# First layer's attention: the values' products of two heads made together, by query tiles, and w_v split earlier

## The chip, the cores and the metric

One Trainium2 chip, one of its cores. The metric is the device time of one execution in microseconds, the median of several runs. The engines are TensorE (PE; its weight loads are shown apart as PEld), VectorE (DVE), ScalarE (ACT), GpSimd (POOL) and SyncE (SP), which here only issues DMAs.

## The reference

Two transformer-like layers on x of 2 batches x 512 tokens x 512 features, float32. The part that the change touches is the first layer's attention, 32 query heads, 8 key/value heads of 128 features, causal:

```
q, k, v = layernorm(x) @ Wq.T, @ Wk.T, @ Wv.T          # q: 32 heads, k and v: 8 heads
q, k = q * cos + rotate_half(q) * sin, k * cos + rotate_half(k) * sin
scores = q k^T / sqrt(128), masked above the diagonal   # each k head serves 4 q heads
out = softmax(scores) v
x = x + layernorm(out @ Wo.T)
```

After it come a linear layer with low-rank additions, a second attention of 32 heads without a mask, and a gated feed-forward layer. They are unchanged.

## The kernel before, in words

Every matrix product is made of three passes (`product`, L81 to L85): each operand is split into a high part, rounded by ACT, and a low part, the rest (`rest`, L90, a subtraction on DVE or POOL). The passes are hi x lo, lo x hi, hi x hi, accumulated in a PSUM bank; L83, L84 and L85 are their lines.

The first layer's attention runs over 8 groups (one k/v head and its 4 q heads each). A group has 8 slots (2 batches x 4 heads) of 4 query tiles of 128 rows: 32 steps, one score tile each. Scores are causal, so tile t has (t + 1) x 128 columns. The groups' passes are software-pipelined: work of a group goes on into the steps of the next one. Step numbers here are taken within a group, modulo 32; "of eight" means modulo 8, since two slots (a pair) repeat every 8 steps.

What is done at which step is written out in plans. `USES0` places the uses of the two general PSUM banks: q of slot s at 4s - 8, its values' product ("pv") at 4s + 21, k of batch b at 16b - 14 (so at steps 18 and 2), v at 16b + 10, v's transposes at 16b + 14. `OUTS0` places the output projection, 4s + t + 26, `LOADS0` the splitting of weights, `FETCH0` their DMAs, 8 steps ahead. Each engine walks through the steps and does, in a fixed order within a step, what the plans give it; engines wait for each other by semaphores.

One slot's way: TensorE makes q, ACT copies it and swaps its halves for the rope (L1775, L1781, L1782), DVE multiplies by the cosine (L1896), POOL by the sine and adds (L2023, L2027), ACT rounds (L1787), POOL makes the low half. TensorE makes the score tile; DVE adds the mask and takes the minimum (L1938), ACT the exponential (L1825), DVE transposes it in blocks of 32 x 32 into `blocks` (L1957). When both slots of a pair are there, SP moves `blocks` to `moved` by 16 DMAs (L1609), which completes the transposition. Both heads of a pair share one buffer of 4 x 5 blocks: the even slot lies above the diagonal, the odd one below. The landed probabilities are rounded by ACT (`landed_hi`, L1832) and their rest made by DVE (even pieces) and POOL (odd pieces), in eight pieces per pair, of 512, 384, 256 and 128 columns for each slot:

```
for lag, pieces in ((LAND0_AT, (0, 1)), (LAND0_AT + 1, (2, 3))):
    slot = m.slot_at(n, lag)
```

so ACT lands at steps 0, 1, 4 and 5 of eight, and DVE and POOL one step later each. POOL's order within a step is: low half of q or k, landed piece, weight's low half, rope. The values' product of one slot has 4 key chunks k; chunk k serves query tiles k to 3, so its three passes have 512, 384, 256 and 128 columns. DVE scales the bank by the inverse sums (L1886), ACT and DVE split it (L1841, L90), and TensorE projects it by w_out into four output banks, one per query tile, which collect 4 heads and are then added to `acc` by DVE (L1973).

Of the kernel before, what the change touches and what calls it, by code (L numbers as in the profile page):

```python
# [23 lines left out]
P = 128  # L24
# [1130 lines left out]
MOVE0_AT, LAND0_AT, PV0_AT, OUT0_AT = 8, 16, 21, 26  # L1155
# [14 lines left out]
class Linear:  # L1170
# [12 lines left out]
    def __init__(self, p, ctx, ctx0, home, banks, xT, acc, ident, half, x_rows, kept):  # L1183
# [7 lines left out]
        self.x_second = self.blocks[:, 0].rearrange("p g c e i -> p (g c e i)")[:, 0:TB * D]            .rearrange("p (t d) -> p t d", t=TB)  # L1191
# [248 lines left out]
def grouped_attention(p, ctx0, xT, acc, ident, half, x_rows, kept, inv_rows, ahead):  # L1440
# [4 lines left out]
    with ExitStack() as ctx:  # L1445
# [8 lines left out]
        NPR, NRAW, TRIANGLES = 2, 5, [P, 2, TB, TB, TB + 1, 32]  # L1454
# [48 lines left out]
        def by_block(rows):  # L1503
            return rows.rearrange("p (g x) -> p g x", g=TB)

# [6 lines left out]
        def chunk_row(rows, slot, e):  # L1512


            return rows[:, :, e, e + 1:TB + 1] if slot % 2 == 0 else rows[:, :, TB - 1 - e, 0:TB - e]

        def chunk_columns(rows, slot, k):

            if slot % 2 == 0:
                return rows[:, :, k, k + 1:TB + 1]  # L1520
            return rows[:, :, k:TB, k]
# [20 lines left out]
        def landing(m, n):  # L1542

            for lag, pieces in ((LAND0_AT, (0, 1)), (LAND0_AT + 1, (2, 3))):
                slot = m.slot_at(n, lag)
                if slot is not None:
                    for e in pieces:
                        yield slot, e
# [16 lines left out]
        def _(sp):  # L1565
            def fetch(m, x, d):
                kind, h = x
                if m is not start:
                    sp.wait_ge(s_w_hi, m.done(FETCH0, x, d) - NRAW)
                    sp.nop(nofuse=True)  # L1570
                    if not (m.first and d == 0):
                        if kind == "wo":
                            sp.wait_ge(s_out, TT + m.done(OUTS0, (GH + h, TB - 1), d - 1))
# [20 lines left out]
            def move(m, pair):  # L1594
# [16 lines left out]
                wait_past(sp, s_inv_dma, m, 32 * (SLOTS // 2), 32 * pair + 16)  # L1611
                sp.dma_start(inv_all[:, k], inv_rows[k].rearrange("p t -> (p t)").unsqueeze(0).to_broadcast([P, P * PAIR]))\
# [37 lines left out]
        def _(pe):  # L1650
            def bank_use(x, m, d, part=range(C)):
# [10 lines left out]
                if kind == "pv":  # L1662
# [5 lines left out]
                    wait_past(pe, s_lo_even, m, 2 * SLOTS, 2 * slot + 2)  # L1668
                    wait_past(pe, s_lo_odd, m, 2 * SLOTS, 2 * slot + 2)
                    for k in range(TB):  # L1670
                        right = Split(chunk_columns(probsT_hi, slot, k),
                                      chunk_columns(probsT_lo[:, slot // 2 % 2], slot, k))
                        last = product(nc, by_block(bank[:])[:, :, k * 32:P].rearrange("p g (t i) -> p g t i", i=32),
                                       v[:, j // GH, k * HD:(k + 1) * HD], right, k == 0, k == TB - 1)
# [31 lines left out]
            def project(m, x, d):  # L1706

                slot, t = x
                h = slot % GH
                if t == 0:  # L1710
                    wait_past(pe, s_o_lo, m, SLOTS, slot + d * SLOTS + 1)
                    if slot < GH:
                        pe.wait_ge(s_w, m.done(LOADS0, ("wo", h), d))
                if h == 0:
                    wait_past(pe, s_added, m, B * TB, TB * (slot // GH + d * B - 1) + t + 1)
                product(nc, out_bank[t][:], oT[:, slot % 2, t * P:(t + 1) * P], w_out[:, h], h == 0, h == GH - 1)\
# [43 lines left out]
        def _(act):  # L1760
# [60 lines left out]
            def exponentials(m, n):  # L1821
# [4 lines left out]
                               bias=negtop[:, n:n + 1], scale=-1.0, accum_out=total[:, n:n + 1]).then_inc(s_exp, 1)  # L1826

            def landed_hi(m, slot, e):
                pair = slot // 2
                if slot % 2 == 0 and e == 0:  # L1830
                    wait_past(act, s_move[pair % 2], m, SLOTS // 4 * MOVES, (pair // 2 + 1) * MOVES)
                act.activation(chunk_row(probsT_hi, slot, e), chunk_row(moved[:, pair % 2], slot, e), ACT.Copy)\  # L1832
                    .then_inc(s_land_hi, 1)
# [9 lines left out]
            def body(m):  # L1843
                for n in m.steps():
# [16 lines left out]
                    for slot, e in landing(m, n):  # L1861
                        landed_hi(m, slot, e)
# [13 lines left out]
        def _(dve):  # L1876
# [71 lines left out]
            def turn_blocks(m, n):  # L1948
# [7 lines left out]
                to = rows[:, :, 0:t + 1, t + 1] if slot % 2 == 0 else rows[:, :, t, 0:t + 1]  # L1956
                dve.transpose(to.rearrange("p c k i -> p k c i"), probs[:, n % NPR, 0:width[t]]).then_inc(s_block, 1)  # L1957

            def landed_lo(m, slot, e):
                wait_past(dve, s_land_hi, m, TILES, TB * slot + e + 1)  # L1960
                k = slot // 2 % 2
                rest(dve, chunk_row(probsT_lo[:, k], slot, e), chunk_row(moved[:, k], slot, e),
                     chunk_row(probsT_hi, slot, e)).then_inc(s_lo_even, 1)
# [5 lines left out]
            def add_rows(m, x, d):  # L1969
                slot, t = x  # L1970
                dve.wait_ge(s_out, TT + m.done(OUTS0, x, d))
                row = slot // GH * TB + t
                dve.tensor_tensor(acc[:, row], out_bank[t][:], acc[:, row], ALU.add).then_inc(s_added, 1)  # L1973
# [4 lines left out]
            def body(m):  # L1978
                for n in m.steps():
# [22 lines left out]
                    for slot, e in landing(m, n - 1):  # L2002
                        if e % 2 == 0:
# [350 lines left out]
```

## Time and profile before

| | |
|---|---|
| time, median of 3 runs (lowest to highest) | 2220.83 us (2217.11 to 2226.0) |
| the profiled execution | 2219.26 us |
| its span | 2217.4 us |
| granted TensorE clock, mean over the span | 0.979 of full |
| TensorE busy | 2095.7 us, 95% |
| DVE, ACT, POOL busy | 76%, 61%, 55% |

The span is that of the instructions in the profile; the execution's time has a little around it. "Busy" of TensorE comes from modelled ends of pipelined matmuls, so the distance from one start to the next tells more than the length. In a timeline each row has the start (us from the span's start), the length, engine and line, operation, output<-inputs, partitions x elements, and in brackets the idle time before it and the instruction that ended it.

### The profile page before, as it was taken

Reading aid. Unit: us, or ns where it says so; the run is one execution under the profiler, and the core shown is the slowest. Engines: PE = TensorE matmul, PEld = TensorE weight load, DVE = VectorE, ACT = ScalarE, POOL = GpSimd, SP = SyncE. Lnnn points to the kernel's source line nnn. Section 1 sums busy time; section 2 is a strip of 40 time slices with the busy share of each in tenths; the row PEclk is TensorE's granted clock in tenths of the full one; section 3 lists DMA queues with packets and bytes.
Section 4 is the critical chain, followed back from the end, with each engine's and each line's share of the span. In section 5 each row is a group of like instructions: output and inputs, shape, how many; then the busy total and the mean of one; then the engine's idle time right before and its main releaser. Section 6 shows DMA issues by size and latency. Waiting matters only on the chain. (4 is left out here: it accounts for less than half of the span.)

```text
span 2217.4 us, 38457 instructions
## 1 busy us (share of the span) xinstructions
PE 2095.7 (95%) x10535; PEld 1765.5 (80%) x10535; DVE 1674.3 (76%) x2972; ACT 1349.9 (61%) x3637; POOL 1223.1 (55%) x985
## 2 busy tenths in 40 slices
PE   6999999999999778999999999999999999968998
PEld 5788888888887657888888888888888888756787
DVE  5778888788788876888878788787877788885322
ACT  5777777777776456666656565665656565554321
POOL 3878787787786555545444554545454553454300
PEclk9999999999999989999999999999999999988999
DMA  2434344434344422444444444444443443433210
GB/s 82 125 105 125 108 104 119 109 109 122 105 118 125 126 69 75 124 99 117 112 105 102 115 106 118 102 100 111 114 106 95 120 108 93 127 113 100 91 53 25
DMA packets 165904, 231.96 MB, mean 105 GB/s; under 512 B 47281, under 2 KB 77137, under 8 KB 165745
## 3 DMA queue, kind: packets, MB, share of 16 engines
q1 hardware_dynamic: 165744, 229.97, 39.5%
q8 instruction: 83, 1.36, 0.3%
q14 instruction: 77, 0.62, 0.1%
HBM read 114.23 MB, written 6.55 MB: 54 GB/s over the span
## 5 line engine op out<-in xcount | busy, mean ns | idle before, releaser
L90 POOL TENSOR_TENSOR l_probsT_lo<-l_moved,l_probsT_hi 128x512 fp32r<-128x512 f32 (+2 forms) x256 | 282.6, 1108 | 307.7 <-ACT l_probsT_hi L940 279.8
L934 ACT ACTIVATE l_probs<-l_score,l_negtop 128x512 f32<-128x512 f32 x256 | 175.8, 687 | 373.8 <-DVE l_negtop L1045 373.0
L90 DVE TENSOR_TENSOR l_probsT_lo<-l_moved,l_probsT_hi 128x512 fp32r<-128x512 f32 (+1 forms) x256 | 288.8, 1128 | 30.9 <-ACT l_probsT_hi L940 30.9
L1045 DVE TENSOR_REDUCE l_negtop<-l_score 128x1 f32<-128x512 f32 x256 | 175.7, 687 | 91.5 <-PE l_score L85 89.2
L1825 ACT ACTIVATE l_probs<-l_score,l_negtop 128x128 f32<-128x128 f32 (+3 forms) x256 | 134.8, 527 | 178.0 <-DVE l_negtop L1938 176.6
L83 PE MATMUL l_score<-l_kT_lo,l_qT_hi 128*128 128x512 f32 (+3 forms) x512 | 191.7, 374 | 42.0 <-POOL l_qT_lo L90 16.8
L83 PE MATMUL l_out<-l_w_out_lo,l_oT_hi 128*128 128x512 f32 x512 | 208.7, 408 | 3.3 <-DVE l_oT_lo L90 2.6
L1938 DVE CUSTOM_DVE_ANT_0 l_score<-l_score,l_mask 128x128 f32<-128x128 f32 (+3 forms) x256 | 126.3, 493 | 107.2 <-PE l_score L85 106.2
L84 PE MATMUL l_out<-l_w_out_hi,l_oT_lo 128*128 128x512 f32 x512 | 201.3, 393 | 0.0
L85 PE MATMUL l_out<-l_w_out_hi,l_oT_hi 128*128 128x512 f32 x512 | 201.1, 393 | 0.0
L83 PE MATMUL l_general<-l_w_qk_lo,xT_hi 128*128 128x512 f32 x504 | 197.4, 392 | 2.5 <-PEq L1445 2.5
L84 PE MATMUL l_general<-l_w_qk_hi,xT_lo 128*128 128x512 f32 x504 | 197.4, 392 | 0.0
L85 PE MATMUL l_general<-l_w_qk_hi,xT_hi 128*128 128x512 f32 x504 | 197.1, 391 | 0.0
L83 PE MATMUL l_general<-l_probsT_lo,l_v_hi 128*128 128x512 f32 (+3 forms) x512 | 182.6, 357 | 13.4 <-POOL l_probsT_lo L90 7.9
L85 PE MATMUL l_general<-l_probsT_hi,l_v_hi 128*128 128x512 f32 (+3 forms) x512 | 185.3, 362 | 0.0
L84 PE MATMUL l_general<-l_probsT_hi,l_v_lo 128*128 128x512 f32 (+3 forms) x512 | 184.9, 361 | 0.0
L85 PE MATMUL l_score<-l_kT_hi,l_qT_hi 128*128 128x512 f32 (+3 forms) x512 | 184.7, 361 | 0.0
L84 PE MATMUL l_score<-l_kT_hi,l_qT_lo 128*128 128x512 f32 (+3 forms) x512 | 184.2, 360 | 0.0
L1060 DVE STREAM_TRANSPOSE l_blocks<-l_probs 128x512 f32<-128x512 f32 x256 | 177.8, 695 | 0.2 <-ACT l_probs L934 0.2
L90 POOL TENSOR_TENSOR l_w_qk_lo<-l_raw_qk,l_w_qk_hi 128x512 fp32r<-128x512 f32 x60 | 77.6, 1294 | 154.6 <-ACT l_w_qk_hi L908 154.6
L640 ACT ACTIVATE l_squares<-l_y 128x128 f32<-128x128 f32 x512 | 151.9, 300 | 10.6 <-DVE l_y L1003 10.6
L83 PEld LDWEIGHTS l_score<-l_kT_lo,l_qT_hi 128*128 128x128 f32 x512 | 96.9, 189 | 69.7 <-ACT l_probs L1825 20.2
(249 smaller groups left out, 6348.6 us busy)
## 6 DMA issues: line engine op xcount, KB each, us to landing
l_moved<-l_blocks SPq DMA_DIRECT2D x1024, 64.0 KB, 2.0
l_moved<-l_blocks SPq DMA_DIRECT2D x512, 80.0 KB, 2.1
l_inv_all<-inv_rows SPq DMA_DIRECT2D x32, 512.0 KB, 4.3
l_raw_out<-l_wo SPq DMA_DIRECT2D x64, 256.0 KB, 4.5
l_inv_all<-inv_rows SPq DMA_DIRECT2D x64, 256.0 KB, 3.7
l_raw_q<-l_wq SPq DMA_DIRECT2D x32, 256.0 KB, 4.3
l_raw_qk<-l_wq SPq DMA_DIRECT2D x64, 128.0 KB, 3.0
l_raw_qk<-l_wk SPq DMA_DIRECT2D x64, 128.0 KB, 3.0
```

The lines of the kernel that those rows point to most:

```text
L83: nc.tensor.matmul(out, left.hi, right.lo, start=first, stop=False, skip_group_check=True)
L84: nc.tensor.matmul(out, left.lo, right.hi, start=False, stop=False, skip_group_check=True)
L85: return nc.tensor.matmul(out, left.hi, right.hi, start=False, stop=last, skip_group_check=True)
L90: return engine.tensor_tensor(out, full, hi.bitcast(F32), ALU.subtract)
L640: last = act.activation(self.squares[:, h], self.y[:, b, t, h * HD:(h + 1) * HD], ACT.Square, accum_out=self.sumsq[:, b, j:j + 1])
L934: act.activation(probs[:, n % NPR], score[n % 2][:], ACT.Exp, bias=negtop[:, n:n + 1], accum_out=total[:, n:n + 1]).then_inc(s_exp, 1)
L1045: dve.tensor_reduce(negtop[:, n:n + 1], score[n % 2][:], AXX, ALU.max, negate=True)\
L1060: dve.transpose(to, probs[:, n % NPR]).then_inc(s_block, 1)
L1825: act.activation(probs[:, n % NPR, 0:width[t]], score[n % 2][:, 0:width[t]], ACT.Exp, bias=negtop[:, n:n + 1], scale=-1.0, accum_out=total ...
L1938: dve.tensor_tensor_reduce(out=score[n % 2][:, 0:w], in0=score[n % 2][:, 0:w], in1=mask[:, S - w:S], scale=-SCALE, scalar=3.0e38, op0=ALU. ...
```

## The change

A pair's two heads are laid out together in 20 blocks (of 32 columns, times 4) instead of two triangles: blocks 0 to 11 hold query tiles 2 and 3 of both heads for key chunks 0 to 2, blocks 12 to 19 the rest. The even slot's bank now takes query tiles 0 and 1 of both heads, the odd slot's bank tiles 2 and 3 of both. The passes of a pair's products are then 512 and 256 columns (even), and 512, 512, 512, 256 (odd): 18 matmuls instead of 24, with the same columns in sum. Landing is done for the pair, in five pieces of 512 columns: ACT at steps 2 (two), 4 (two) and 5 of eight, DVE pieces 1, 2, 4 and POOL pieces 0, 3 one step later. The output projection takes the heads in the new order, so w_out of odd heads is needed 2 steps and split 1 step sooner, and the additions to `acc` fall in other steps. w_v's split moves from step 4 to step 0. Fetches stand 7 steps ahead of the splits instead of 8. SP's moves wait for TensorE's product (`s_bank`) instead of DVE's scaling (`s_free`), which now only the broadcast of the inverse sums waits for; ACT waits for the pair before's odd product ahead of its first piece.

```diff
-MOVE0_AT, LAND0_AT, PV0_AT, OUT0_AT = 8, 16, 21, 26
+MOVE0_AT, PV0_AT, OUT0_AT = 8, 21, 26
+LAND0_AT = {18: (0, 1), 20: (2, 3), 21: (4,)}
+PIECES0, EVEN0, ODD0 = 5, (1, 2, 4), (0, 3)
...
-LOADS0 = {("wq", h): 4 * h - 13 for h in range(GH)} | {("wo", h): 4 * h + 22 for h in range(GH)}
-LOADS0 |= {("wk", 0): -19, ("wv", 0): 4}
-FETCH0 = Plan({x: n - 8 for x, n in LOADS0.items()})
+LOADS0 = {("wq", h): 4 * h - 13 for h in range(GH)} | {("wo", h): 4 * h + 22 - h % 2 for h in range(GH)}
+LOADS0 |= {("wk", 0): -19, ("wv", 0): 0}
+FETCH0 = Plan({x: n - 7 for x, n in LOADS0.items()})
...
-        NPR, NRAW, TRIANGLES = 2, 5, [P, 2, TB, TB, TB + 1, 32]
+        NPR, NRAW, TRIANGLES = 2, 5, [P, 2, TB, TB * (TB + 1), 32]
...
+        def cells(slot, t):
+            h = slot % 2
+            if t >= 2:
+                return slice(2 * h + t - 2, 4 * t + 2 * h + t - 1, 4)
+            at = (12, 16)[t] + 2 * h
+            return slice(at, at + t + 1)
+
+        def piece(rows, e):
+            return rows[:, :, 4 * e - 8:4 * e - 4] if e >= 2 else rows[:, :, 12 + 4 * e:16 + 4 * e]
+
+        def column(n):
+            slot, t = divmod(n, TB)
+            return slot // 2 * PAIR + (2 * t + slot % 2 if t < 2 else TB + 2 * (slot % 2) + t - 2)
+
+        PV = ([(0, slice(12, 19, 2), slice(0, 4)), (1, slice(17, 20, 2), slice(2, 4))],
+              [(k, slice(4 * k, 4 * k + 4), slice(0, 4)) for k in range(TB - 1)] + [(3, slice(13, 16, 2), slice(1, 4, 2))])
+
+        def out_item(slot, n):
+            return (n % 2, n // 2, n % 2 * 2 + n // 2) if slot % 2 == 0 else (2 + n % 2, n // 2, n)
...
-                if not (m.first and pair < 2):
-                    was = 2 * pair - 3
-                    sp.wait_ge(s_free, m.done(USES0, ("pv", was % SLOTS), was // SLOTS, of_dve))
+                    sp.wait_ge(s_bank, m.done(USES0, ("pv", was % SLOTS), was // SLOTS))
...
-                    for k in range(TB):
-                        right = Split(chunk_columns(probsT_hi, slot, k),
-                                      chunk_columns(probsT_lo[:, slot // 2 % 2], slot, k))
+                    for k, at, to in PV[odd]:
+                        right = Split(probsT_hi[:, :, at], probsT_lo[:, pair % 2, :, at])
...
+            def landed_hi(m, pair, e):
+                if e == 0:
+                    if not (m.first and pair == 0):
+                        was = 2 * pair - 1
+                        act.wait_ge(s_bank, m.done(USES0, ("pv", was % SLOTS), was // SLOTS))
+                        act.nop(nofuse=True)
+                    wait_past(act, s_move[pair % 2], m, SLOTS // 4 * MOVES, (pair // 2 + 1) * MOVES)
+                act.activation(piece(probsT_hi, e), piece(moved[:, pair % 2], e), ACT.Copy).then_inc(s_land_hi, 1)
...
             def add_rows(m, x, d):
-                slot, t = x
-                dve.wait_ge(s_out, TT + m.done(OUTS0, x, d))
+                slot, n = x
+                t, of, _ = out_item(slot, n)
+                if slot % GH // 2 * 2 + of == GH - 1:
+                    dve.wait_ge(s_out, TT + m.done(OUTS0, x, d))
```

## Rows read from the trace of the kernel before

**Rows 1.** The page, part 1: busy time of each engine, its share, instructions.
```profile
PE 2095.7 (95%) x10535; PEld 1765.5 (80%) x10535; DVE 1674.3 (76%) x2972; ACT 1349.9 (61%) x3637; POOL 1223.1 (55%) x985
```

**Rows 2.** Timeline of TensorE at steps 8 and 24: start us, length, instruction, [idle before, releaser].
```profile
312.26 0.32 PE L83 MATMUL l_score<-l_kT_lo,l_qT_hi 128*128 128x128 f32 x1 [1.54 <-POOL l_qT_lo L90]
...
355.36 0.39 PE L85 MATMUL l_general<-xT_hi,l_w_q_hi 128*128 128x512 f32 x1
356.21 0.32 PE L83 MATMUL l_score<-l_kT_lo,l_qT_hi 128*128 128x128 f32 x1 [0.46 <-POOL l_qT_lo L90]
...
399.35 0.39 PE L85 MATMUL l_general<-xT_hi,l_w_q_hi 128*128 128x512 f32 x1
401.27 0.32 PE L83 MATMUL l_score<-l_kT_lo,l_qT_hi 128*128 128x128 f32 x1 [1.54 <-POOL l_qT_lo L90]
```

**Rows 3.** Timeline of TensorE through one value product of before and the next matmuls.
```profile
404.11 0.40 PE L83 MATMUL l_general<-l_probsT_lo,l_v_hi 128*128 128x512 f32 x1
...
404.81 0.34 PE L83 MATMUL l_general<-l_probsT_lo,l_v_hi 128*128 128x384 f32 x1
...
405.34 0.28 PE L83 MATMUL l_general<-l_probsT_lo,l_v_hi 128*128 128x256 f32 x1
...
405.69 0.22 PE L83 MATMUL l_general<-l_probsT_lo,l_v_hi 128*128 128x128 f32 x1
...
405.97 0.45 PE L83 MATMUL l_out<-l_w_out_lo,l_oT_hi 128*128 128x512 f32 x1
406.26 0.40 PE L84 MATMUL l_out<-l_w_out_hi,l_oT_lo 128*128 128x512 f32 x1
```

**Rows 4.** Timeline of ACT from step 18 to step 20.
```profile
342.42 0.58 ACT L1825 ACTIVATE l_probs<-l_score,l_negtop 128x384 f32<-128x384 f32 x1 [2.79 <-DVE l_negtop L1938]
...
344.41 0.60 ACT L1775 ACTIVATE l_rope<-l_general 128x512 f32<-128x512 f32 x1
345.31 0.69 ACT L1825 ACTIVATE l_probs<-l_score,l_negtop 128x512 f32<-128x512 f32 x1 [0.30 <-DVE l_negtop L1938]
...
347.23 0.37 ACT L1825 ACTIVATE l_probs<-l_score,l_negtop 128x128 f32<-128x128 f32 x1
...
349.01 1.05 ACT L1832 ACTIVATE l_probsT_hi<-l_moved 128x512 fp32r<-128x512 f32 x2
```

**Rows 5.** Timeline of POOL from step 21 to the q of step 24.
```profile
350.13 1.37 POOL L90 TENSOR_TENSOR l_probsT_lo<-l_moved,l_probsT_hi 128x384 fp32r<-128x384 f32 x1 [1.20 <-ACT l_probsT_hi L1832]
351.46 1.74 POOL L2023 TENSOR_TENSOR l_rope<-l_rope,l_trig 128x512 f32<-128x512 f32 x1
...
354.61 1.47 POOL L90 TENSOR_TENSOR l_qT_lo<-l_rope,l_qT_hi 128x512 fp32r<-128x512 f32 x1
```

**Rows 6.** Timelines of POOL (first row) and DVE around step 20.
```profile
347.64 1.30 POOL L90 TENSOR_TENSOR l_w_q_lo<-l_raw_q,l_w_q_hi 128x512 fp32r<-128x512 f32 x1
...
345.63 0.68 DVE L1896 TENSOR_TENSOR l_rope<-l_rope,l_trig 128x512 f32<-128x512 f32 x1
...
347.69 1.80 DVE L90 TENSOR_TENSOR l_oT_lo<-l_scaled,l_oT_hi 128x512 fp32r<-128x512 f32 x1
```

**Rows 7.** Groups by form, 150 to 750 us: count, busy us, mean ns, idle before.
```profile
L90 POOL TENSOR_TENSOR l_probsT_lo<-l_moved,l_probsT_hi 128x384 fp32r<-128x384 f32 x55 | 68.9, 1252 | 26.0 <-ACT l_probsT_hi L1832 26.0
...
L1832 ACT ACTIVATE l_probsT_hi<-l_moved 128x512 fp32r<-128x512 f32 x55 | 34.3, 624 | 5.3 <-DMA l_moved<-l_blocks 5.0
```

**Rows 8.** Timeline of POOL from step 5 to the q of step 8.
```profile
394.15 1.24 POOL L90 TENSOR_TENSOR l_probsT_lo<-l_moved,l_probsT_hi 128x384 fp32r<-128x384 f32 x1 [0.35 <-ACT l_probsT_hi L1832]
395.35 1.75 POOL L90 TENSOR_TENSOR l_w_v_lo<-l_raw_v,l_w_v_hi 128x512 fp32r<-128x512 f32 x1
...
399.88 1.26 POOL L90 TENSOR_TENSOR l_qT_lo<-l_rope,l_qT_hi 128x512 fp32r<-128x512 f32 x1
```

**Rows 9.** Timeline of SP's queue, last group's last pair.
```profile
732.52 0.33 SPq L1600 DMA_DIRECT2D inv_rows<-l_inv  x1
734.59 10.88 SPq L1609 DMA_DIRECT2D l_moved<-l_blocks  x16
```

More of the change, by code:

```diff
@@ L1542, in landing @@
         def landing(m, n):
-            for lag, pieces in ((LAND0_AT, (0, 1)), (LAND0_AT + 1, (2, 3))):
+            for lag, pieces in LAND0_AT.items():
                 slot = m.slot_at(n, lag)
-                if slot is not None:
+                if slot is not None and slot % 2 == 0:
                     for e in pieces:
-                        yield slot, e
+                        yield slot // 2, e
         def pair_at(m, n):
@@ L1611, in move @@
                 wait_past(sp, s_inv_dma, m, 32 * (SLOTS // 2), 32 * pair + 16)
+                if not (m.first and pair < 2):
+                    sp.nop(nofuse=True)
+                    sp.wait_ge(s_free, m.done(USES0, ("pv", was % SLOTS), was // SLOTS, of_dve))
                 sp.dma_start(inv_all[:, k], inv_rows[k].rearrange("p t -> (p t)").unsqueeze(0).to_broadcast([P, P * PAIR]))\
@@ L1860, in body @@
                             output_hi(m, x, d)
-                    for slot, e in landing(m, n):
-                        landed_hi(m, slot, e)
+                    for pair, e in landing(m, n):
+                        landed_hi(m, pair, e)
                     for x, d in m.turns(USES0, n, 5):
@@ L1955, in turn_blocks, with landed_lo @@
                 rows = blocks[:, pair % 2]
[L1956 to L1963, printed above, removed]
+                dve.transpose(rows[:, :, cells(slot, t)].rearrange("p c k i -> p k c i"), probs[:, n % NPR, 0:width[t]]).then_inc(s_block, 1)
+            def landed_lo(m, pair, e):
+                wait_past(dve, s_land_hi, m, PIECES0 * SLOTS // 2, PIECES0 * pair + e + 1)
+                k = pair % 2
+                rest(dve, piece(probsT_lo[:, k], e), piece(moved[:, k], e), piece(probsT_hi, e)).then_inc(s_lo_even, 1)
             def output_lo(m, slot):
@@ L2001, in body @@
                             rope_cos(x, m, d)
-                    for slot, e in landing(m, n - 1):
-                        if e % 2 == 0:
-                            landed_lo(m, slot, e)
+                    for pair, e in landing(m, n - 1):
+                        if e in EVEN0:
+                            landed_lo(m, pair, e)
                     for x, d in m.turns(OUTS0, n):
-                        if x[0] % GH == GH - 1:
-                            add_rows(m, x, d)
+                        add_rows(m, x, d)
                     if m.last:
@@ L2032, in rope_lo, with landed_lo @@
                 rest(pool, to.lo, rope[:, rope_at(m, x, d)[0], 0], to.hi).then_inc(s_rope_lo, 1)
-            def landed_lo(m, slot, e):
-                wait_past(pool, s_land_hi, m, TILES, TB * slot + e + 1)
-                k = slot // 2 % 2
-                rest(pool, chunk_row(probsT_lo[:, k], slot, e), chunk_row(moved[:, k], slot, e),
-                     chunk_row(probsT_hi, slot, e)).then_inc(s_lo_odd, 1)
+            def landed_lo(m, pair, e):
+                wait_past(pool, s_land_hi, m, PIECES0 * SLOTS // 2, PIECES0 * pair + e + 1)
+                k = pair % 2
+                rest(pool, piece(probsT_lo[:, k], e), piece(moved[:, k], e), piece(probsT_hi, e)).then_inc(s_lo_odd, 1)
             for t in range(TT):
@@ L2053, in body @@
                             rope_lo(x, m, d)
-                    for slot, e in landing(m, n - 1):
-                        if e % 2:
-                            landed_lo(m, slot, e)
+                    for pair, e in landing(m, n - 1):
+                        if e in ODD0:
+                            landed_lo(m, pair, e)
                     for x, d in m.turns(LOADS0, n, 1):
```

45 lines of the change are left out of this document (17 added, 28 removed).

## The prediction

> **What bounds the kernel now.** I read the page's busy table first: TensorE (PE) is busy for 95% of the span, VectorE (DVE) 76%, ScalarE (ACT) 61%, GpSimd (POOL) 55% [rows 1]. The edit touches only the first layer's attention. Its rhythm can be read from TensorE's timeline: step 8 of two neighbouring groups begins at 312.26 and 401.27, so a group of 32 steps takes 89.0 us, and eight groups take some 712 of the 2217 us [rows 2]. Inside a group matmuls follow each other without a hole except in two places. At step 8 TensorE's last matmul before the score starts at 399.35; one such matmul takes about 0.23, so the score could start at 399.58 and starts at 401.27: 1.69 us lost. At step 24 it is 355.36 + 0.23 = 355.59 against 356.21: 0.62 lost [rows 2]. Both rows name the same releaser, the low half of q, made on POOL. So the layer is bound by TensorE's instruction stream plus two waits on POOL, 2.3 us in every 89. These are the two steps for which k's rope is made as well (k at steps 18 and 2, its rope on POOL at 21 and 5), in front of that q.
>
> **The products.** I take the cadence, start to start, not the modelled durations. In a value product of before, three matmuls of 512 columns take 404.81 - 404.11 = 0.70, three of 384 take 0.53, three of 256 take 0.35, three of 128 take 0.28, and the next one, of 512, is held for 0.29 instead of 0.23, which I charge to the 128s: 0.34. That is 1.92 per head, 3.84 per pair [rows 3]. Three narrow ones thus cost what three of 256 do. The change keeps the columns and regroups them: the even slot's bank takes 3 of 512 and 3 of 256 (0.70 + 0.35 = 1.05), the odd slot's 9 of 512 and 3 of 256 (2.45), together 3.50. TensorE saves 0.34 per pair, 32 pairs, 10.9 us. But the saving is uneven: the even slot's product (steps 5, 13, 21, 29) shrinks by 0.87, the odd one's (1, 9, 17, 25) grows by 0.53. The two losing steps, 8 and 24, lie behind an even product. Whatever POOL does at 5 to 7, TensorE now asks for the q 0.87 sooner, and if POOL is not quicker, that much turns into waiting. The new order reads blocks of 32 columns that lie apart; the old order read such blocks for its odd heads too, so I charge nothing.
>
> **The landing, ACT.** Before, a pair's probabilities were rounded in eight pieces (512, 384, 256, 128 columns for each head) at steps 0, 1, 4, 5 of eight; now in five of 512 at steps 2, 2, 4, 4, 5. Columns are equal and three instructions fall away, but step 2 gains two pieces that it did not have. At step 18 ACT has no room for them: it waits until 342.42 for the score's top, and then runs without a hole: exponential, swap of q, copy of k at 344.41, exponential 19 at 345.31 (after 0.30 of waiting), exponential 20 at 347.23, swap of k, two pieces from 349.01 to 350.06 [rows 4]. Two pieces of 0.62 (the mean of a landing piece of 512, [rows 7]), overlapping by a tenth, make 1.15. Put in ahead of the copy they move it to 345.56 and exponential 19 to 346.1: the 0.30 is used up and 0.8 stays. The next two pieces (512 and 512 for 512 and 384) end 0.1 later still. Here lies the price of the later landing: POOL's piece of step 21 waits for the second of them.
>
> **The landing, POOL and DVE.** At step 21 POOL starts its piece at 350.13, after 1.20 of idle time until ACT delivered, and then has k's two rope instructions and q's low half, which ends at 354.61 + 1.47 = 356.08; 0.13 later the score starts [rows 5]. All of it is in one queue, 5.95 us long. A piece of 512 in place of 384 adds 0.3 (a split of 512 alone takes 1.30, row 347.64 in [rows 6]; the 384s took 1.25 on average, collisions included, in [rows 7], and 1.0 is 1.30 by columns and a fixed part). So with ACT's delay alone q's half comes 0.8 + 0.1 + 0.3 = 1.2 us later. That is the lower bound for this chain. The upper one comes from DVE's new piece at step 3 of eight, which stands ahead of the mask and minimum of the next score. POOL now works on its own new piece at that time (345.05 to 346.35) and then on q's rope. DVE and POOL hold each other up: DVE's oT low half took 1.80 us from 347.69, beginning just after POOL's weight split at 347.64 (1.30 long), against 0.68 for the uncontended cosine of 345.63, and ended 0.55 after POOL did [rows 6]. Taking the same for the new order, DVE's cosine waits to 346.9, POOL's rope runs to 348.2, DVE's piece ends 348.8, the score's minimum 349.2, and exponential 20 starts at 349.3 instead of 347.23. POOL's piece then starts 2.1 later than before; plus 0.3 for its width, less 0.5 for a collision that its rope had (1.74 at 351.46, 1.30 alone) and need not have again: 1.9 [rows 5]. The trace has no row for that order, so both ends are kept: +1.2 to +1.9 at step 24. I take 1.55, between the ends, since the waits are shown but their order in the new kernel is not. The Trainium skill says of this pair (SBUF — State Buffer, "Who interferes with whom") that a VectorE instruction with two inputs in SBUF and a GpSimd instruction that reads SBUF exclude each other for the whole instruction; by that rule the upper end holds, and the trace agrees in the 1.80 us row.
>
> **The sum for the half group with step 24.** TensorE's stretch from score 18 to score 24 grows by 1.2 to 1.9 (its own 0.87 is lost in the longer wait). Steps 17 and 25 add 0.53 each, step 29 saves 0.87. Together +1.4 to +2.1.
>
> **The v weight.** POOL's split of w_v takes 1.75 us at 395.35 and stands between the piece at 394.15 and k's rope, ahead of the q that step 8 waits for, which ends at 399.88 + 1.26 = 401.14 [rows 8]. It goes to step 1, where POOL has no landing any more. So step 8's chain loses 1.75. It gains ACT's and DVE's delay as at step 24 (between 1.0 and 2.1, since POOL waited only 0.35 there), and 0.3 for the wider piece: -0.4 to +0.6. The half group: that, plus 0.53 twice, less 0.87: -0.2 to +0.8. A group thus grows by 1.2 to 2.9, I take 2.0. Seven groups have each chain: +14 us (+8.5 to +20). The first group has no landing at step 8 and so gets the w_v gain alone, and the last has no k rope at 24: together -1 us.
>
> **Costed at nothing.** The moves from blocks to moved are as many and as long (16 issues, 10 to 11 us on SP). They now wait for the product instead of its scaling. In the last group that frees SP at about 732.9 (inv_rows is issued at 732.52) instead of 734.59 [rows 9]: up to -1.7 there, but landing's first pieces come two steps later in a tail of norms on DVE; I set 0, bounds -2 and +2. In the loop their start 4 us sooner covers the weights' fetches, queued behind them on SP: w_v, now needed at step 0 and not 4, is issued after the moves of step 24, and without that head start it would come in the same microseconds as its use. Fetches of wq0 and wo0 wait for output products of the same step, before a move that waits for DVE anyway. ACT's new wait for the odd product stands behind an exponential that needs a later score: covered. The accumulations moved from steps 6 to 9 to 4, 5, 8, 9 add 0.68 before two minimums on DVE; ACT is later still there.
>
> **Result.** The profiled execution took 2219.26 us (span 2217.4 and 1.9 around it); it is 1.6 under the median of 2220.83. 2219.3 + 14 - 1 = 2232; against the median 2234.
>
> **Rivals.** *POOL was the queue, and w_v's removal opens it* (faster). If ACT delivers its pieces of steps 4 and 20 no later than before (POOL waited 0.35 and 1.20 for them), all of w_v's 1.75 is gained (0.53 + 0.53 - 0.87 - 1.75 = -1.56 for that half), and the other half keeps its wait of 0.62 (-0.68): -2.2 per group, 7 groups, -16 us: 2205. For it: the long queue in [rows 8]. Against it: ACT's only idle time from 342.42 to 350.06 is the 0.30 [rows 4]. It decides where ACT's delay is under 0.35. *A wash:* the q of step 24 comes as before relative to score 18 (+0.19), that of step 8 gains half of w_v's 1.75: -0.5 per group, 2217, down to 2212 if all of it. *The port never collides* and step 8's chain is at its low end: +1.2 per group, 2229. *Both instructions exclude each other at every step*, the rule quoted above taken to its end: +2.9 per group, plus small waits at step 0 where q's slack is under 1 us: 2243 to 2249. *It doesn't do what it says* (narrow products cost nothing now): the cadence of 128s, 0.34 for three, excludes it.
>
> **Chances and range.** Forecast (2232 to 2242) 0.46; port at every step (2242 to 2250) 0.14; collision-free (2223 to 2231) 0.20; wash 0.10; faster 0.10. About half a per cent, 11 us, is what a measurement of this kernel can tell from no change. Slower by more: 0.60, within: 0.30, faster: 0.10. The range 2217 to 2249 leaves out the faster rival and half of the wash; the forecast's own is 2232 to 2242.
>
> **What would show it.** Group period 90.2 to 91.9 instead of 89.0; 18 matmuls per pair and none of 128 columns among the value products; the wait before score 24 at 2.5 or more, that before score 8 between 1.2 and 2.5; exponential 20 (of 128 columns) 0.8 to 2 us later behind score 18; DVE's piece at step 19 over 1.2 us long. I am wrong if the waits at 8 and 24 stay at or under 2.3 in sum.

## The result, and the profile after

The changed kernel takes 2250.49 us (median of 4 runs, 2248.6 to 2253.08) against 2220.76 beside it: 1.0134 of before, 95% interval 1.0116 to 1.0152, 30 us slower. The direction was forecast (+14), the size was not: 2234 stood against 2250.5, and the range ended at 2249. The profiled execution took 2250.93 us, its span is 2249.1 ([rows 1] is the same line of before):

```profile
PE 2103.7 (94%) x10343; PEld 1751.7 (78%) x10343; DVE 1689.1 (75%) x2940; ACT 1339.6 (60%) x3541; POOL 1218.1 (54%) x921
```

The 192 matmuls fewer are there. TensorE is busy 8 us longer all the same, which already says that some of its matmuls took longer.

**Where the time went.** The starts of the first layer's 256 score tiles are all in both traces, so each step has an interval, from the start of its score to the start of the next. Means over groups 2 to 6, in us (their sum, "group", is called the period below); steps that are not listed differ by 0.02 at most:

| interval from step | 0 | 1, 17 | 5, 13, 21, 29 | 6, 22 | 7 | 8 | 9 | 15 | 23 | 24 | 25 | 31 | group |
|---|---|---|---|---|---|---|---|---|---|---|---|---|---|
| before | 3.75 | 4.35 | 2.99 | 1.22 | 4.44 | 2.50 | 4.33 | 2.74 | 3.37 | 2.52 | 4.33 | 1.38 | 88.97 |
| after | 3.87 | 4.83 | 2.11 | 2.15 | 5.29 | 3.40 | 4.86 | 3.11 | 5.30 | 4.14 | 5.05 | 2.19 | 96.13 |

A group grew by 7.2 us where 2.0 was forecast. The layer's last score starts at 771.38 instead of 724.83, 46.6 us later. Of this the total shows 30: the second attention layer, which no line of the change touches, became faster. From its first to its last score minimum it takes 1083.2 us instead of 1100.4 (139.3 us in each full group against 141.0 to 143.2). So two effects of opposite sign have to be explained.

**The waits.** TensorE's timeline of after, around step 24 (first five rows) and step 8 of the next group, which answer to [rows 2]:

```profile
368.91 0.50 PE L83 MATMUL l_score<-l_kT_lo,l_qT_hi 128*128 128x512 f32 x1 [0.77 <-ACT l_probs L1842]
...
374.21 0.47 PE L83 MATMUL l_score<-l_kT_lo,l_qT_hi 128*128 128x128 f32 x1 [2.28 <-POOL l_qT_lo L90]
...
375.43 0.63 PE L84 MATMUL l_general<-xT_hi,l_w_q_lo 128*128 128x512 f32 x1
375.86 0.63 PE L85 MATMUL l_general<-xT_hi,l_w_q_hi 128*128 128x512 f32 x1
376.29 0.63 PE L83 MATMUL l_general<-xT_lo,l_w_q_hi 128*128 128x512 f32 x1
...
422.70 0.32 PE L83 MATMUL l_score<-l_kT_lo,l_qT_hi 128*128 128x128 f32 x1 [2.27 <-POOL l_qT_lo L90]
...
423.60 0.40 PE L85 MATMUL l_general<-xT_hi,l_w_q_hi 128*128 128x512 f32 x1
423.83 0.40 PE L83 MATMUL l_general<-xT_lo,l_w_q_hi 128*128 128x512 f32 x1
```

Before both scores TensorE now loses 2.43 us (2.66 from start to start, less 0.23 for a matmul), where before it was 1.69 and 0.62. Such a stretch without a matmul is called a hole below and given from start to start. One step ahead of each TensorE waits for an exponential, which is new. Now read the distance of the matmuls behind the wait: 0.43 us at 375.43, 0.23 at 423.60. After the first of the two equal waits TensorE runs at half its clock for some 3 us, after the second it doesn't. The windows of two neighbouring groups show it as a whole (length, busy times with counts, then the granted clock, the DMA share, GB/s):

```profile
300.30:396.74 96.44, 89.63 (x417) 73.98 (x417) 77.17 (x149) 64.35 (x147) 69.31 (x48) 0.96 0.40 103
396.74:491.68 94.94, 88.14 (x416) 72.65 (x417) 76.52 (x149) 64.23 (x147) 69.30 (x48) 0.98 0.40 105
```

Before, every group from 2 to 6 has granted clock 1.00. In after it falls behind score 24 in all five of them and behind score 8 in three.

**The chain to score 24.** ACT, DVE and POOL of after in the same half group (answering to [rows 4 to 6]):

```profile
358.43 0.58 ACT L1842 ACTIVATE l_probs<-l_score,l_negtop 128x384 f32<-128x384 f32 x1 [2.88 <-DVE l_negtop L1957]
...
360.42 1.15 ACT L1852 ACTIVATE l_probsT_hi<-l_moved 128x512 fp32r<-128x512 f32 x2
361.48 0.58 ACT L1792 ACTIVATE l_rope<-l_general 128x512 f32<-128x512 f32 x1
361.95 0.68 ACT L1842 ACTIVATE l_probs<-l_score,l_negtop 128x512 f32<-128x512 f32 x1
...
364.98 0.37 ACT L1842 ACTIVATE l_probs<-l_score,l_negtop 128x128 f32<-128x128 f32 x1 [1.22 <-DVE l_negtop L1957]
...
366.76 1.16 ACT L1852 ACTIVATE l_probsT_hi<-l_moved 128x512 fp32r<-128x512 f32 x2
...
368.30 0.46 ACT L1842 ACTIVATE l_probs<-l_score,l_negtop 128x256 f32<-128x256 f32 x1
```

```profile
361.64 1.33 DVE L1915 TENSOR_TENSOR l_rope<-l_rope,l_trig 128x512 f32<-128x512 f32 x1
362.90 1.78 DVE L90 TENSOR_TENSOR l_probsT_lo<-l_moved,l_probsT_hi 128x512 fp32r<-128x512 f32 x1
364.60 0.29 DVE L1957 CUSTOM_DVE_ANT_0 l_score<-l_score,l_mask 128x128 f32<-128x128 f32 x1
...
372.22 0.73 DVE L90 TENSOR_TENSOR l_probsT_lo<-l_moved,l_probsT_hi 128x512 fp32r<-128x512 f32 x1
```

```profile
368.00 1.27 POOL L90 TENSOR_TENSOR l_probsT_lo<-l_moved,l_probsT_hi 128x512 fp32r<-128x512 f32 x1 [0.46 <-ACT l_probsT_hi L1852]
369.22 1.75 POOL L2041 TENSOR_TENSOR l_rope<-l_rope,l_trig 128x512 f32<-128x512 f32 x1
371.12 1.28 POOL L2045 TENSOR_TENSOR l_rope<-l_rope 128x512 f32<-128x512 f32 x1
372.37 1.71 POOL L90 TENSOR_TENSOR l_qT_lo<-l_rope,l_qT_hi 128x512 fp32r<-128x512 f32 x1
```

This is the forecast's upper path. Cosine 1.33 and DVE's piece 1.78 us long, where POOL works too (the same piece with 0.73 at 372.22), minimum 20 behind it, exponential 20 1.74 later behind exponential 18 than before (6.55 against 347.23 - 342.42 = 4.81), ACT's pieces at 366.76, POOL's at 368.00, and q's low half ready at 374.08. At 368.30 a price that the forecast left out can be read: exponential 21 stands behind swaps, two pieces and a copy, and score 23 (368.91) needs the bank that it frees.

### The profile page after: what moved, and what is told of

Read it like the earlier page. It is cut to its first block and busy times, and to the rows that moved or that the text cites. A ratio compares the mean times of both kernels' runs of the same rounds, so it can differ in the third digit from the quotient of the medians.

```text
span 2249.1 us, 37941 instructions
## 1 busy us (share of the span) xinstructions
PE 2103.7 (94%) x10343; PEld 1751.7 (78%) x10343; DVE 1689.1 (75%) x2940; ACT 1339.6 (60%) x3541; POOL 1218.1 (54%) x921
## 3 DMA queue, kind: packets, MB, share of 16 engines
HBM read 114.23 MB, written 6.55 MB: 54 GB/s over the span
## 5 line engine op out<-in xcount | busy, mean ns | idle before, releaser
L90 POOL TENSOR_TENSOR l_probsT_lo<-l_moved,l_probsT_hi 128x512 fp32r<-128x512 f32 x192 | 254.9, 1333 | 401.0 <-ACT l_probsT_hi L940 263.8
L90 DVE TENSOR_TENSOR l_probsT_lo<-l_moved,l_probsT_hi 128x512 fp32r<-128x512 f32 x224 | 308.8, 1379 | 32.3 <-ACT l_probsT_hi L940 32.1
L83 PE MATMUL l_general<-l_probsT_lo,l_v_hi 128*128 128x512 f32 x448 | 172.7, 386 | 15.2 <-POOL l_probsT_lo L90 7.9
L84 PE MATMUL l_general<-l_probsT_hi,l_v_lo 128*128 128x512 f32 x448 | 172.0, 384 | 0.0
L85 PE MATMUL l_general<-l_probsT_hi,l_v_hi 128*128 128x512 f32 x448 | 171.5, 383 | 0.0
```

The source lines that it names most:

```text
L83: nc.tensor.matmul(out, left.hi, right.lo, start=first, stop=False, skip_group_check=True)
L84: nc.tensor.matmul(out, left.lo, right.hi, start=False, stop=False, skip_group_check=True)
L85: return nc.tensor.matmul(out, left.hi, right.hi, start=False, stop=last, skip_group_check=True)
L90: return engine.tensor_tensor(out, full, hi.bitcast(F32), ALU.subtract)
```

## Experiments

Layer one's period is the measure below; the total holds the second layer too. Four small edits of a few lines, condensed:

```diff
 # k's rope late (POOL)
-for x, d in m.turns(USES0, n, 3):
-    if x[0] in QK: rope_add(x, m, d)
+for x, d in m.turns(USES0, n, 3):
+    if x[0] == "q": rope_add(x, m, d)
+for x, d in m.turns(USES0, n, 4):
+    if x[0] == "k": rope_add(x, m, d)
 # spread / middle landing
-LAND0_AT = {18: (0, 1), 20: (2, 3), 21: (4,)}
+LAND0_AT = {18: (0, 1), 21: (2,), 22: (3,), 23: (4,)}
+LAND0_AT = {18: (0, 1), 20: (2,), 21: (3,), 22: (4,)}
 # DVE's pieces behind the next minimum
 tops(m, n)
+for pair, e in landing(m, n - 2):
+    if e in EVEN0: landed_lo(m, pair, e)
...
-for pair, e in landing(m, n - 1):
-    if e in EVEN0: landed_lo(m, pair, e)
```

**1. k's rope late, on the kernel after.**

> The kernel after, with POOL making the sine product and the sum of k's rope one step later (steps 22 and 6), so that they stand behind the low half of q that steps 24 and 8 wait for. Theory, the queue on POOL and the clock: in the kernel after TensorE loses 2.43 us before each of these two scores, and in the steps right behind them about 2.7 us per group to a granted clock of 1.2 GHz. Without k's rope (3.0 us) in front, the low half of q is ready about when it is asked for, so both go: group period 96.1 less 4.9 less 2.7 = 88.5 us, and about 2250 - 53 = 2197 in all. Rival one, ACT delivers q's high half too late: the wait stays over 1.5 us and the period over 94. Rival two, the clock falls for the denser stream of 512 columns, waits or not: the waits go, the 2.7 stays, period 91.2, about 2216.

2206.8 us, 0.9944 of before (0.9925 to 0.9963): 44 us less than after. Period 89.7, granted clock 1.00 in the groups. The interval of step 7 falls from 5.29 to 2.85, of 23 from 5.30 to 2.86. So the queue on POOL made the two waits. The 1.2 us over the expected 88.5 is mostly ACT: the waits of 0.93 for its exponential remain, and 0.46 each before scores 9 and 25 appear.

```profile
351.48 1.27 POOL L90 TENSOR_TENSOR l_probsT_lo<-l_moved,l_probsT_hi 128x512 fp32r<-128x512 f32 x1 [0.46 <-ACT l_probsT_hi L1852]
353.46 1.29 POOL L90 TENSOR_TENSOR l_qT_lo<-l_rope,l_qT_hi 128x512 fp32r<-128x512 f32 x1 [0.71 <-ACT l_qT_hi L1804]
```

POOL's timeline there: the low half follows the piece at once, 2.0 us behind it instead of 4.4.

**2. The same on the kernel before.**

> The kernel before, with k's rope one step later on POOL and nothing else. The two waits of before (1.69 and 0.62 us per group) go: period 89.0 less 2.3 = 86.7 us, about 2205 in all. If ACT or DVE set the time of q's low half instead of POOL's queue, the period stays within 0.5 us of 89.

2204.0 us, 0.9921 (0.9904 to 0.9937), period 87.1. As expected, but 0.3 us are lost at each of steps 9 and 25.

**3. The landing spread.**

> The kernel after, with the landing pieces 2, 3 and 4 of a pair at steps 5, 6 and 7 of eight in place of 4, 4 and 5. Theory: ACT's two pieces at step 4 hold back the exponential that frees the bank for the score of step 7 (0.93 us lost there twice per group), and POOL's piece at step 5 stands ahead of q's low half. The first wait goes; TensorE then asks for q 0.93 sooner and POOL has it 1.3 sooner, so that 2.0 of the 2.43 us stay, or about 1.2 if POOL's later instructions also no longer collide. Group period 96.1 less 1.9 less 0.9 to 2.5 = 91.7 to 93.3 with the clock as it is, and 2.7 less of that if a wait of 1.2 no longer lets the clock fall: 89 to 93, 2200 to 2229. Rival, the two pieces are not what the score of step 7 waits for (DVE's minimum is): its wait of 0.93 stays and the period is 94 or more.

A miss: 2335.0 us, 1.0518 (1.05 to 1.0535), period 105.7. The waits of steps 6 and 22 went (1.28), so they hang on ACT's two pieces at step 4 of eight, and those of 8 and 24 shrank; but the odd products' intervals (1, 9, 17, 25) rose from 4.83 to between 8.2 and 10.1, and the granted clock of a group is 0.95. TensorE's timeline:

```profile
405.25 0.32 PE L83 MATMUL l_score<-l_kT_lo,l_qT_hi 128*128 128x128 f32 x1 [1.49 <-POOL l_qT_lo L90]
...
410.43 0.49 PE L83 MATMUL l_general<-l_probsT_lo,l_v_hi 128*128 128x512 f32 x1 [2.15 <-DVE l_probsT_lo L90]
```

DVE's last piece was late (the [2.15] at 410.43), which I had not costed. With k's rope late as well:

> The kernel after with both edits, the spread landing and k's rope behind q's low half. Theory: none of the three waits is left, nor a fall of the clock: period 96.1 less 1.9 less 4.9 less 2.7 = 86.6 us, 2184 in all. It should then lie about 1.4 us per group under the kernel before with k's rope late, which is what the regrouped products save on TensorE. Rival, the regrouped products save nothing once waits are away: 88 us per group or more.

2330.7 us (1.0488, 1.0471 to 1.0506), period 105.8: nothing gained in a group, since the products' waits now rule. The middle way:

> The kernel after with k's rope late and the landing pieces 2, 3, 4 at steps 4, 5 and 6 of eight (the spread one had 5, 6, 7, and its odd products waited 3.4 us for DVE's last piece). With k's rope late alone the group takes 89.7 us, of which 0.93 twice is TensorE's wait for ACT's exponential at steps 7 and 23, and 0.4 twice a like one at steps 9 and 25. Theory: two pieces in one step of ACT make these waits; with one piece per step they go and no product waits for a piece: period 87.0 to 87.8, about 2190 in all. Rival: DVE's last piece, one step later, now holds the odd product as in the spread landing: period over 91.

2225.3 us (1.0025, 1.0015 to 1.0034), period 92.6 where 87.0 to 87.8 was expected: the rival held. Steps 1, 9, 17 and 25 take 5.8 to 6.6 instead of 4.8. The landing of the change has no slack towards its own odd product: one step later costs more than the exponentials' waits.

**4. The v weight, alone and taken back.**

> The kernel before with only the v weight's part of the change: w_v split at step 0 in place of 4, fetches 7 steps ahead. Theory: POOL's split of w_v (1.75 us) leaves the queue in front of the q of step 8, so the 1.69 us lost there go: period 89.0 less 1.7 = 87.3, 12 us less in all, 2209. Rival: another engine sets that q, or w_v's fetch is late where it now stands: period 88.5 to 90.

2214.2 us, 0.9972 (0.9959 to 0.9984), period 88.3: step 7's interval falls by 1.17, not 1.69, and step 1's rises by 0.48, where TensorE waits for ACT, which now rounds w_v ahead of its copy (L1775).

> The kernel after with w_v's split back at step 4. Theory: the wait before score 8 grows by the 1.3 to 1.75 us of the split, from 2.43 to about 4, and the clock falls behind it in every group instead of in some: period 96.1 plus 1.5 plus 0.6 = 98.2, 2265 in all. If w_v at step 0 was itself a cost (in the waits before the scores of steps 0 and 16), the period moves by less than 0.7.

2270.5 us, 1.0224 (1.0205 to 1.0243), period 98.9. That part of the change saves 20 us inside it, since a split in that queue costs waiting and clock.

**5. DVE's pieces behind the minimum.**

> The kernel after, with DVE making its landed pieces behind the mask and minimum of the next score instead of ahead of them. This takes apart the forecast's upper price for step 24's chain. Theory, the piece ahead of the minimum: the minimum of score 20 comes about 1.4 us sooner, exponential 20 with it, ACT's next two pieces and POOL's piece of step 21 follow, and the wait before scores 24 and 8 falls from 2.43 to 1.0 to 1.5, and the falls of the clock behind them go; period 96.1 less 2.0 to 2.8 less up to 2.7 = 90.6 to 94. Rival: ACT's own two pieces at step 2 of eight set exponential 20, and the order on DVE is worth under 0.5 us per step: period over 94.5. An opposite price: products of steps 5 and 1 now wait for pieces that come later.

2231.0 us, 1.0049 (1.0031 to 1.0067), period 93.4. Exponential 20 starts 6.72 behind score 18 instead of 8.04, so the piece ahead of the minimum was worth 1.3 us. It reaches TensorE at step 8 (interval 7 falls by 0.97; behind the hole of 1.69 us that is left the clock falls no more, 2.49 for 3.40) and removes the waits of 6 and 22, but score 24 starts no sooner (6.17 for 5.30, with 22 down by 0.87). There POOL is full:

```profile
450.57 1.75 POOL L90 TENSOR_TENSOR l_w_q_lo<-l_raw_q,l_w_q_hi 128x512 fp32r<-128x512 f32 x1
452.28 1.78 POOL L90 TENSOR_TENSOR l_probsT_lo<-l_moved,l_probsT_hi 128x512 fp32r<-128x512 f32 x1
454.03 1.74 POOL L2041 TENSOR_TENSOR l_rope<-l_rope,l_trig 128x512 f32<-128x512 f32 x1
```

No brackets, so no idle time, and each takes 1.75 where an undisturbed one takes 1.3.

**6. Is it the hole that lets the clock fall?**

```diff
+wait_past(pe, s_exp, m, TILES, n - 1)
+if n in (8, 24):
+    for _ in range(8):
+        nc.tensor.matmul(score[n % 2][:], xT.hi[:, 0, 0:P], xT.hi[:, 0, 0:S], start=True, stop=True)
 if t == 0: pe.wait_ge(s_rope_lo, ...)
-wait_past(pe, s_exp, m, TILES, n - 1)
```

The wait for the exponential moves ahead, since the added matmuls write the score's bank.

> The kernel after with 8 additional matmuls of 512 columns (results overwritten) on TensorE right ahead of its wait for q's low half at steps 8 and 24: 8 x 0.23 = 1.84 us of work inside the 2.43 us that it waits there. Nothing that is computed or waited for changes. Theory, the granted clock falls because TensorE stands still there: with the hole cut to about 0.6 the clock stays at 2.4 GHz, granted clock 1.00 in the windows of the groups, and the period is 96.1 less 2.7 = 93.4 us. Rival, the clock falls for the density of the stream or by chance: still 95 to 98, or more with the added work. The extra 96 instructions or so ahead of the second layer move its loop again, so the first layer's period decides and not the whole time.

2228.3 us, 1.0036 (1.0019 to 1.0053): 22 us less than after, with more work. Period 93.2, granted clock 1.00 in the groups; TensorE's timeline:

```profile
460.35 2.06 PE L1755 MATMUL l_score<-xT_hi 128*128 128x512 f32 x8
462.74 0.33 PE L83 MATMUL l_score<-l_kT_lo,l_qT_hi 128*128 128x128 f32 x1 [0.34 <-POOL l_qT_lo L90]
```

The score starts as late as ever; only the steps behind it changed (8: 3.40 to 2.51, 24: 4.14 to 2.49, 25: 5.05 to 4.83). The hole lets the clock fall, at 2.9 us per group. Of the 22 us some 19 lie in the first layer (its last score starts at 752.52 instead of 771.38); the other 3.4 lie in the second, which differs by as much between two profiles of after's own program (experiment 7).

**7. The second layer.** In before's second layer TensorE stops at the start of five groups, for 2.15 to 2.48 us from start to start, and waits for nothing that the profile shows; behind four of these stops matmuls run at half the clock. In after there is none. One of them:

```profile
1396.71 0.69 PE L83 MATMUL l_score<-l_kT_lo,l_qT_hi 128*128 128x512 f32 x1 [1.92 <-issue]
1397.20 0.63 PE L84 MATMUL l_score<-l_kT_hi,l_qT_lo 128*128 128x512 f32 x1
```

The page's part 3 gives the queue q8 for instructions 83 packets and 1.36 MB in before, 37 and 0.61 in after; by their times nine fall in each such group of before, and none between 1146.8 and 1865.5 in after. The five stops make 10.9 of the 17.2 us, the lower clock behind them the rest. So: is it the place of the loop in the program?

> The kernel after with 144 no-operations on TensorE's queue ahead of the second attention layer, which stands unchanged in both kernels but takes 139.3 us per group after and 143.2 before. That is about the number of TensorE instructions that the change took out of the program ahead of it (72 matmuls with their weight loads). Theory: where the second layer's loop lies in the program decides whether its instructions are loaded again in each pass; with the 144 put back they are: its period 143.2 again, seven loads of nine packets on the instruction queue, and 3.9 times 6 or 7 = 23 to 27 us less the ends: 2268 to 2277 in all, with a few us for the no-operations themselves. Rival: the second layer is slower before for a reason of timing carried over from the first (phase of DMAs, clock): 139.3 stays, 2250 to 2255.

> The kernel before with 112 no-operations on TensorE's queue ahead of the second attention layer, which brings its loop to the same place within blocks of 256 instructions as in the kernel after. Theory: the second layer's period falls from 143.2 to 139.3 us, and the whole to about 2221 - 20 = 2200. Rival, as for the padded kernel after: 143.2 stays and the whole is 2221 to 2226.

Void: the no-operations left no instruction in either program (2251.5 and 2221.0 us; 1.0137, 1.011 to 1.0163, and 1.0001, 0.9989 to 1.0013; 37 and 83 packets). They still give a second profile of each program. That of after has a period of 95.5 in place of 96.1, since the clock falls behind score 8 in two of five groups and not in three, and its second layer takes 1079.8 us. With matmuls instead:

> The kernel after with 72 additional matmuls of 32 columns (results overwritten) right ahead of the second attention layer on TensorE. The no-operations of the padded kernels left no instruction in the program, so that question stayed open; these stay, 144 instructions with their weight loads, which is what the change took out ahead of that layer. Theory, the place of the loop in the program: the second layer's period is 143.2 us again instead of 139.3 and the instruction queue q8 shows about 80 packets instead of 37: 2250 + 23 + about 5 for the matmuls = 2278. Rival, it is not the place (another part of the program or the timing): 37 packets, 139.3, about 2255.

> The kernel before with 56 such matmuls at the same place, 112 instructions, which with the 144 that the change removed make 256, the size of 16 KB in instructions of 64 bytes as the packets of that queue suggest (1.36 MB in 83). Theory, the place within such blocks: period of the second layer 139.3 in place of 143.2, 37 packets in place of 83, and 2220 - 20 + 4 = 2204 in all. Rival, the place is not what matters, or it is the absolute place and not that within a block: 143.2, 83 packets, about 2224.

2285.9 us (1.029, 1.0266 to 1.0314): 83 packets, the five stops, groups of 141.0 to 143.3. And 2217.5 us (0.9985, 0.9975 to 0.9995): 38 packets, no stop, 139.3. It is the place. The inserted matmuls themselves cost more than I expected, 12 us for 56, and hid the gain in the second. So they went where TensorE is idle:

> The kernel before with 56 very small matmuls (32 x 8, results overwritten) at the very start of TensorE's program, where it stands idle for 10.7 us until the first norm. It moves everything behind by 112 instructions at no cost in time, where the 56 matmuls ahead of the second layer took 12 us. Theory, place of the loop: the second layer's period 139.3 us, 37 or 38 packets on q8, the first layer's 89.0, and in all 2220 less 18 to 21 = about 2201. Rival: the first layer's loop, moved as well, now is the one that is loaded again; then its period rises above 90.

> The kernel before with k's rope late on POOL and the 56 small matmuls at the start: no regrouped products, no new landing, no earlier v weight. If the two gains (16 and 18 to 20 us) add, 2184 to 2188, which would be under the kernel after with its two edits (2200.8), and say that the regrouped products bring nothing in this form. If they don't add: 2195 or more.

2207.0 us (0.9923, 0.9903 to 0.9943) and 2189.3 us (0.9848, 0.9833 to 0.9864); 39 packets in both. The fp32 matmuls appear as 112, not 56, so the shift was 224 instructions; that place serves too. The gains add up, and this is the fastest kernel of the study, without any of the change.

**8. Both edits that helped, on either kernel.**

> The kernel after with both edits that helped alone: k's rope behind q's low half on POOL, and DVE's landed pieces behind the next minimum. With k's rope late, 89.7 us per group, TensorE still waits 0.93 twice (steps 7, 23) and 0.46 twice (9, 25) for exponentials of ACT; the other edit took the 0.93 away. Theory, the waits of the second kind come from DVE's pieces ahead of the minimum: they go and nothing else appears, 89.7 less 1.9 less 0.5 to 0.9 = 86.9 to 87.3, 2187 to 2192 in all, the fastest kernel of all. Rival: as at step 24 of the other edit alone, POOL's queue is full by then and gives the time back in another wait: period 88.5 or more.

> The kernel before with the same two edits: the fair partner of the last one. Before with k's rope late has 87.1 us per group and a wait of about 0.3 left at steps 9 and 25. Expected 86.4 to 87.1, 2197 to 2204 in all (its second layer keeps its 143.2 us). If the regrouped products save 0.34 per pair once nothing waits, the kernel after with both edits lies 1.4 us per group under this one in its first layer; the rival is that its later landing takes that back even then, and the two are within 0.5.

The first: 2200.8 us, 0.9902 (0.9886 to 0.9918), faster than both kernels, period 88.9 where 87 was expected; the gain at 6 and 22 comes back at step 31 (3.32 for 2.26), a wait for POOL. Behind this hole of 2.2 us the clock fell in one of the five groups, which took 90.2; the others took 88.6. The second: 2219.8 us (0.9991, 0.9978 to 1.0004), 89.2, worse than with k's rope late alone (87.1): here DVE's order costs 2.1 us per group. So the two are no fair pair; the fair one is the best order of each, 88.9 against 87.1.

## Why the prediction was right in direction and wrong in size

Two steps of it failed. The sum priced a wait of TensorE at its length and put what the clock does behind it at nothing, without a reason: 2.7 us per group. And step 8's chain, priced at +0.1 us, measured +0.9. Smaller misses are the waits before scores 16 and 0 (1.3 for nothing) and step 24's chain (0.4).

- **The products.** Right to 0.05 us: -0.88 at 5, 13, 21, 29 (forecast -0.87) and +0.48 to +0.53 at 1, 9 and 17 (0.53). But no kernel of the study turned the 10.9 us into time: the best with the regrouping has 88.9 us per group, the best without it 87.1.
- **Step 24's chain.** Forecast +1.2 to +1.9, taken 1.55. From score 18 to score 24 it is +1.99 by the table. The piece ahead of the minimum is worth 1.3 (experiment 5). POOL's piece starts 1.86 later behind score 18 (11.06 for 9.20; the upper path had 2.1). It is no longer for its width (1.27 for 1.37, where 0.3 was added), but k's rope collided again (1.75, where 0.5 was taken off), and q's low half takes 1.71 instead of 1.47 [rows 5], beside DVE's last piece.
- **Step 8's chain.** This term was mis-sized: forecast -0.4 to +0.6, taken 0.1, measured +0.90 from score 2 to score 8. POOL's piece starts 1.8 later behind score 2 (11.05 against 9.24 in before), w_v gives back 1.37 of its 1.75, since k's rope behind it now takes 3.1 in place of 2.8, and q's low half takes 1.71 where it took 1.26 [rows 8]. POOL in after, step 5 to the q of step 8 (score 2 starts at 405.45):

```profile
416.50 1.27 POOL L90 TENSOR_TENSOR l_probsT_lo<-l_moved,l_probsT_hi 128x512 fp32r<-128x512 f32 x1 [2.16 <-ACT l_probsT_hi L1852]
417.73 1.74 POOL L2041 TENSOR_TENSOR l_rope<-l_rope,l_trig 128x512 f32<-128x512 f32 x1
419.61 1.28 POOL L2045 TENSOR_TENSOR l_rope<-l_rope 128x512 f32<-128x512 f32 x1
420.86 1.71 POOL L90 TENSOR_TENSOR l_qT_lo<-l_rope,l_qT_hi 128x512 fp32r<-128x512 f32 x1
```

- **The half groups' savings at 13 and 29.** They were booked in full. Scores 16 and 0 now wait for POOL's q as well, 0.37 and 0.81. At step 0 POOL's split of w_q and its piece take 1.75 each at 391.92 and 393.62, and the low half ends at 396.61, 0.13 before score 0; in before it ended at 375.91, 0.9 before it. The prediction named such waits only in a rival.
- **The clock was not in the sum at all.** 2.7 us per group by the table (0.90 at 8, 1.62 at 24, 0.2 at 25), shown by experiment 6; in the second profile of the same program it is 2.2. It is the largest term of the miss. Behind the hole of before (1.92) the clock never fell; behind that of after (2.66) it fell in 8 of the 10 cases, and in 7 of 10 in each of two more profiles with the same first layer (the no-operations and the matmuls on after).
- **The sum then closes.** 2.0 forecast, +0.4 and +0.8 for the chains, +1.3 for scores 16 and 0 (0.1 of it at step 0 itself), +2.7 for the clock: 7.2 us per group, as measured.
- **The second layer** was nowhere in the forecast: -17.2 us, by the place of its loop. Without it the change would have been 47 us slower. That 2250 lies so near to the forecast is luck.
- **Rivals.** "Both exclude each other at every step" came nearest, in place and in size, yet for +2.9 per group. "POOL was the queue, w_v opens it" is out: w_v alone gives 6 us, and taking it back costs 20, but the later landing refills the queue. Of the signs, the wait before score 24 was 2.43 for "2.5 or more" and the period 96.1 for 90.2 to 91.9; the wait before score 8 (2.43), exponential 20 (1.74 later) and DVE's piece (1.78 long) came as said.
- **Costed at nothing.** ACT's wait for the odd product and SP's moves do not show in TensorE's waits, which name only POOL's q and ACT's exponential in a group. That the exponential itself would be late was missed: ACT's idle 0.30 was used for exponential 19, and not asked again for 21, where TensorE's own shorter product asks 0.88 sooner.

On the port the Trainium skill (SBUF — State Buffer, "Who interferes with whom") says that a VectorE instruction with two SBUF inputs and a GpSimd instruction that reads SBUF contend for a port that only one can hold. The traces agree where both run: 1.78 against 0.73 us on DVE, 1.75 against 1.3 on POOL. On the second layer it says (Runtime: NRT & Kernel Launch, "Instruction fetch mechanics") that instructions come in blocks of 16 KB, and that a branch whose target is not held forces a load. The packets are of that size (1.36 MB in 83), and the stops stand where the loop branches back, as that rule would have it. That the loop's code is loaded in every pass at one place of the program and in none at another is what the runs show; how many blocks are held they do not settle.

## What to carry to other kernels

A stage whose engine already waits gains nothing from less work on that engine: first ask what each wait hangs on and what stands ahead of it in that queue, and move that (here a rope that nobody awaited yet: 16 us in before, 44 in after, for a few lines). A wait on TensorE must be priced with what comes behind it: here 2.4 us lost before a score brought some 1.7 more at the low clock in eight cases of ten. A regrouping that asks for its inputs at other steps can cost more than it saves: no order of the landing tried here turned the saving into time. And before a small difference is put down to an edit, look at stages that the edit doesn't touch: the place of a loop alone was worth 17 us, more than most edits.

## What was not expected of the hardware

- Two equal holes of 2.66 us, start to start: one followed by 3 us at 1.2 GHz, the other not. Of the holes of 2.66 in three profiles 22 of 30 were, of those of 2.2 in the last kernel of the change one of five, of those of 1.92 none. Dummy matmuls in the hole kept the clock and made the kernel 22 us faster.
- A loop of 736 matmuls per pass ran without one packet on the instruction queue, or with nine per pass and a stop of 2.15 to 2.48 us, depending on 112 to 224 instructions ahead of it.
- Matmuls of 32 columns, inserted behind a stop of 2.75 us, started 0.21 us apart (56 in 12 us); 112 records of 8 columns at the start took 6.1.
